# Taking the small extra matmuls out of attention and out of the output projection

## What is computed

```python
# attention, 16 heads of 64; n is normalised twice
xn = layernorm(layernorm(x)) * gamma
q, k, v = heads(xn @ Wq), heads(xn @ Wk), heads(xn @ Wv)
q, k = rotary(q) * 64 ** -0.5, rotary(k)
sim = q @ (k @ W_bilinear).T
x = x + merge(softmax(sim) @ v) @ Wo
# 8 experts, all computed for all tokens, two of them weighted in
xt = layernorm(x)
w, idx = top_k(xt @ Wg.T + bg, 2); w = softmax(w)
h = relu(xt @ W1[e].T + b1[e])
x = x + sum over e of comb[:, e] * (h @ W2[e].T + b2[e])
```

## Time and profile before

| what | value |
|---|---|
| median of 3 runs | 5789.53 us (5823.94, 5595.1, 5789.53) |
| profiled execution, its own time | 5596.39 us |
| its span on the slowest core | 5594.5 us (the eight cores: 5580.3 to 5594.5) |
| PE busy | 4492.4 us, 80% |
| ACT busy | 1806.0 us, 32% |
| DVE busy | 1051.8 us, 19% |
| mean granted TensorE clock | 0.707 of full |

### The profile page before, as it was taken

How to read it: one execution, slowest core, us unless ns; L and a number is a source line. 1 busy time by engine, 2 the same in 40 slices (tenths; PEclk the granted TensorE clock), 3 DMA queues, 4 the chain that set the end, 5 groups by cost and what they waited for, 6 DMA issues and landing times. The chain is left out here.

```text
span 5594.5 us, 49207 instructions; the slowest of 8 cores (5580.3 to 5594.5 us)
## 1 busy us (share of the span) xinstructions
PE 4492.4 (80%) x17554; PEld 1579.7 (28%) x17554; DVE 1051.8 (19%) x2222; ACT 1806.0 (32%) x2827; POOL 41.6 (1%) x66
## 2 busy tenths in 40 slices
PE   3445379999999543699999997529999999999999
PEld 1111112222222111122222222214444444444444
DVE  3343421000000334200000003440111111010101
ACT  1110135666656211266665662002121111212121
POOL 0000000000000000000000000000000000000000
PEclk8666655555555566655555555759999999999999
DMA  3223100000000232000000000600303203023031
GB/s 64 51 44 57 30 8 1 1 1 1 1 1 1 60 60 53 15 1 1 1 1 1 1 1 0 135 0 1 61 1 61 46 16 61 12 49 61 1 76 46
DMA packets 34702, 150.48 MB, mean 27 GB/s; under 512 B 2828, under 2 KB 2957, under 8 KB 32294
## 3 DMA queue, kind: packets, MB, share of 16 engines
q0 software_dynamic: 23952, 111.51, 11.6%
q1 hardware_dynamic: 10518, 35.83, 2.0%
HBM read 250.39 MB, written 8.39 MB: 46 GB/s over the span
## 5 line engine op out<-in xcount | busy, mean ns | idle before, releaser
L607 ACT ACTIVATE arena<-pb,arena 128x512 bf16<-128x512 f32 x2048 | 1287.4, 683 | 857.7 <-PE pb L596 857.7
L622 PE MATMUL pb<-arena 128*128 128x512 bf16 x2048 | 1246.1, 608 | 39.0 <-ACT arena L607 38.9
L970 PE MATMUL pb<-arena 128*128 128x512 bf16 x4096 | 894.0, 379 | 33.0 <-ACT arena L951 27.5
L944 PE MATMUL pb<-arena 128*128 128x512 bf16 x4096 | 891.2, 380 | 1.2 <-DMA arena<-w1t 1.1
L951 ACT ACTIVATE arena<-pb,arena 128x512 bf16<-128x512 f32 x512 | 351.8, 687 | 1446.9 <-PE pb L944 1446.9
L596 PE MATMUL pb<-arena 64*128 64x512 bf16 x2048 | 611.1, 605 | 0.0
L970 PEld LDWEIGHTS pb<-arena 128*128 128x128 bf16 x4096 | 396.4, 98 | 523.2 <-issue 54.2
L944 PEld LDWEIGHTS pb<-arena 128*128 128x128 bf16 x4096 | 400.4, 98 | 486.5 <-issue 5.7
L986 DVE SCALAR_TENSOR_TENSOR arena<-pb,arena 128x512 f32<-128x512 f32 x256 | 192.2, 751 | 1631.6 <-PE pb L970 1414.3
L626 PE MATMUL pb<-arena 1*1 1x64 bf16 x2048 | 424.0, 207 | 0.0
L640 DVE COPY arena<-pb 1x512 f32<-1x512 f32 x64 | 44.1, 689 | 1959.4 <-PE pb L622 1959.4
(11 more groups left out here) (136 smaller groups left out, 1522.5 us busy)
## 6 DMA issues: line engine op xcount, KB each, us to landing
arena<-wkv POOLq DMA_DIRECT2D x32, 1024.0 KB, 9.3
arena<-w1t POOLq DMA_DIRECT2D x8, 4096.0 KB, 27.2
arena<-w2t POOLq DMA_DIRECT2D x8, 4096.0 KB, 27.2
arena<-x_roll SPq DMA_DIRECT2D x48, 512.0 KB, 3.5
arena<-wq POOLq DMA_DIRECT2D x8, 1024.0 KB, 9.4
out<-arena SPq DMA_DIRECT2D x16, 512.0 KB, 2.6
arena<-wo POOLq DMA_DIRECT2D x1, 2048.0 KB, 20.4
arena<-costab SPq DMA_DIRECT2D x2, 512.0 KB, 5.2
```

The costliest lines, as they stand in the source:

```text
L607: l_exp = P.op("scalar", (lambda sb, pt, pr: lambda e: e.activation(out=pt, in_=pb[sb][:, :], func=AF.Exp, bias=s_bias[:, biascol + pr: bi ...
L622: e.matmul(pb[ob][0:128, :], a_v[:, js * VTW + h * (DH + 1): js * VTW + h * (DH + 1) + 128], pt, start=(js == 0), stop=(js == 15)),
L944: e.matmul(pb[b][:, :], f_w1[:, d * HID + hf * 128: d * HID + (hf + 1) * 128], f_ln2T[:, d * OWN + tc * 512: d * OWN + (tc + 1) * 512], st ...
L970: last = e.matmul(pb[b][:, :], f_hT[:, hf * 512 + m4 * 128: hf * 512 + (m4 + 1) * 128], f_w2[:, hf * D + oh * 512: hf * D + (oh + 1) * 512 ...
```

## The change

The small matmul behind each value matmul goes (two in each round, 2048 in all), and the one behind each group of the output projection (32 in all). The value matmul and the last matmul of a group still carry the signals. `warm_burst` stays. Nothing else differs; below L626 the changed file's lines have other numbers (L788 becomes L786).

```diff
-                            l_av = P.op("tensor", (lambda ob, h, pt, js: lambda e: (
+                            l_av = P.op("tensor", (lambda ob, h, pt, js: lambda e:
                                 e.matmul(pb[ob][0:128, :],
                                          a_v[:, js * VTW + h * (DH + 1):
                                              js * VTW + h * (DH + 1) + 128],
-                                         pt, start=(js == 0), stop=(js == 15)),
-                                e.matmul(pb[7][0:1, 0:64], c_ones128b[0:1, 0:1],
-                                         c_ones128b[0:1, 0:64], start=True,
-                                         stop=True))[0])(ob, h, pt, js),
+                                         pt, start=(js == 0), stop=(js == 15)))(
+                                             ob, h, pt, js),
...
-                lm = P.op("tensor", (lambda m, oh, b: lambda e: (
-                    [e.matmul(pb[b][:, :],
+                lm = P.op("tensor", (lambda m, oh, b: lambda e: [
+                    e.matmul(pb[b][:, :],
...
-                     for c in range(8)],
-                    e.matmul(pb[7][0:1, 0:64], c_ones128b[0:1, 0:1],
-                             c_ones128b[0:1, 0:64], start=True, stop=True))[0][-1])(m, oh, b),
+                    for c in range(8)][-1])(m, oh, b),
```

More of the change, by code:

```diff
@@ L786, in build_nc @@
                 b = (m * 2 + oh) % 4
-                lm = P.op("tensor", (lambda m, oh, b: lambda e: (
-                    [e.matmul(pb[b][:, :],
-                              a_aoT[:, c * OWN + m * 128: c * OWN + (m + 1) * 128],
-                              r_wo[:, c * D + oh * 512: c * D + (oh + 1) * 512],
-                              start=(c == 0), stop=(c == 7))
-                     for c in range(8)],
-                    e.matmul(pb[7][0:1, 0:64], c_ones128b[0:1, 0:1],
-                             c_ones128b[0:1, 0:64], start=True, stop=True))[0][-1])(m, oh, b),
+                lm = P.op("tensor", (lambda m, oh, b: lambda e: [
+                    e.matmul(pb[b][:, :],
+                             a_aoT[:, c * OWN + m * 128: c * OWN + (m + 1) * 128],
+                             r_wo[:, c * D + oh * 512: c * D + (oh + 1) * 512],
+                             start=(c == 0), stop=(c == 7))
+                    for c in range(8)][-1])(m, oh, b),
                     waits=[l_wo, bank_owner.get(b)], signal=L(tag))
```

## The result

| | before | after |
|---|---|---|
| median of 10 runs each | 5808.82 us (5595.07 to 5866.76) | 5045.56 us (4932.2 to 5356.96) |
| profiled execution | 5596.39 us | 4933.2 us |
| span of the slowest core | 5594.5 us | 4931.3 us |
| mean granted TensorE clock | 0.707 | 0.844 |

The account below looks back on a forecast made before the run. PE at half clock was taken to bound attention; 659 us from 64 blocks at 10.3 each and 8 us from the output projection, off 5596.4, gave 4930 us, range 4840 to 5300.

Parts of the forecast that it names:

- The bound: Attention: waits for PE at half clock, granted 0.50, with PE busy 94% and 33.39 us a block.
- The round at the low clock: Attention, one key tile: 1.90 us becomes 0.54 + 0.43 + 0.54 = 1.51 us, 0.39 less.
- bare-load rival: Attention at the low clock: weight loads stay bare, 0.28 us less a round, 287 + 8 gained, 5301 us; chance 0.06.
- The clock: Attention: denser full-height work raises the clock to 1.00 in most of each block; 4930 us, chance 0.62.
- rival of the low clock: Attention's clock stays low: gain 403 + 8 = 411 us, time 5185 us; chance 0.26.
- The round at full clock: Attention at 1.00: PE needs 0.89 us a round, so ACT's two exponentials bound it at 1.154 us.
- The loss at the change of blocks: Between attention blocks: 3.7 us at full clock, plus 0.9 us for a low-clock stretch, making 23.1 us a block.
- The low stretch: Attention, after most changes of blocks: 4 us of rounds at the low clock, costing 0.9 us a block.
- some 3 us: PE pauses this long at each change of blocks, so the clock will fall at most of these pauses.
- Output projection: Groups of eight L788 go from 1.95 to 1.70 us; 32 x 0.25 = 8 us gained, full clock kept.
- the rival on the slower side: Denser attention makes the experts' clock fall; at 0.75 they lose 606 us, time 5907 us; chance 0.03.

Follow-up runs that it names:

- run with small matmuls of full height: Kernel before, with the small matmul behind each value matmul given weights of 128 rows and 128 columns instead of one-row, one-column form; 4956.7 us.
- the two runs that kept one small matmul: Changed kernel with one small matmul a round put back: between the two value matmuls, 5261.2 us; between the second and the next scores, 4979 us by cores 0 to 3.
- projection's part alone: Kernel before, with only the 32 small matmuls L793 of the output projection taken out; 5591.2 us.
- run with 7 and 4 fillers: Changed kernel plus 7 full-height matmuls behind each block's last value matmul and 4 ahead of its first; 4858.9 us.
- run with the second small matmul kept: Changed kernel with the small matmul between the second value matmul and the next scores put back; 4979 us by cores 0 to 3.
- the full-height burst: Kernel before, with non-zero data in pass 0's one-row burst and 24 matmuls of 128 rows and 128 columns as pass 1's burst; 5581.6 us.

## Why the prediction was right, by its own steps

**The bound.** PE at a granted clock of 0.50 set attention's pace. With PE's work per round cut and its clock raised, the block fell from 33.37 to 23.17 us, and ACT took over in the rounds at full clock.

**The round at the low clock.** 1.51 us, forecast 1.51. Its parts are, by the median of the starts in the changed kernel's trace, 0.54 from the scores to L622, 0.40 to the second L622 and 0.56 to the scores, forecast 0.54, 0.43 and 0.54. The second L622's load is hidden: 0.40 us is no more than the 0.427 at which L449 follow each other at a granted clock of 0.50 (kernel before, 262.9 to 265.6 us). The bare-load rival is out. Equal shapes behave so in the run with small matmuls of full height too, where L622 takes 0.40 us to the matmul behind it. No run tells how the loads are hidden.

**The clock.** This was a judgement with a chance of 0.62, and it held; it falls at the changes of blocks as forecast, at 30 of 31. That one-row work does nothing for the clock, and that it is the form of the small matmuls and not their number that counts, is shown by two runs: full-height small matmuls leave the clock at 0.87, as without any, and a one-row burst leaves it at 0.50 with zeros as data and with others. That they act by the gaps they put between full-height work fits the two runs that kept one small matmul: with 1.65 us a round the clock mostly comes back, with 1.76 us only in part. It is not shown apart from the place of the small matmul. Of the full gain of 663 us, what the instructions cost at the low clock was forecast as 411 us (rival of the low clock). No run held the denser round at the low clock, so the split is by forecast alone; the low rounds measured at 1.51 us support it.

**The round at full clock.** 1.16 us, forecast 1.154. The spacings of 0.427 and 0.213 us for 512 columns were reckoned from GHz, while the traces give the clock as a share of full: they show 0.427 us at 0.50 (the L449 above) and 0.216 at 1.00 (L788, projection's part alone).

**The loss at the change of blocks.** Two terms were off, in opposite directions. The change itself is 3.2 us, forecast 3.7. Most of the difference is one reading: the 2.46 us from the end of L622 to the next scores came from rows at the low clock, and the eight transposes L647 in it are faster at the full one. Before, and in the run with 7 and 4 fillers, where they are L649:

```profile
809.23 0.98 PE L647 MATMUL pb<-arena 1*128 1x1 f32 x8 [1.41 <-DVE arena L641]
...
863.45 0.62 PE L649 MATMUL pb<-arena 1*128 1x1 f32 x8
...
864.01 0.61 PE L597 MATMUL pb<-arena 64*128 64x512 bf16 x4
```

From the transposes to the scores is 810.14 - 809.23 = 0.91 us before and 864.01 - 863.45 = 0.56 us at full clock, 0.35 us less. The low stretch costs 23.17 - 21.79 = 1.4 us a block, forecast 0.9: I took 4 us of rounds at the low clock, and 0.27 of a block is 6.3 us. About 0.2 us of the 1.4 lies in the change itself, where a low clock slows the transposes and the scores (4.19 us on average from the last exponential to the next block's first, 3.96 with the fillers); the rest lies in the rounds. PE's pause of "some 3 us" is two in the trace after, 1.61 us ahead of L645 and 0.61 us ahead of the first L622. Together 4.6 and 4.6. Here the forecast of 4930 had luck, about 0.5 us x 64 = 32 us in each direction.

**Output projection.** 6.0 to 6.5 us, forecast 8. The full clock was taken for all of it, and its first group or two run at the low one.

**The experts' clock.** They ran at 1.00 and 1818.7 us, so the rival on the slower side did not come true in the execution compared, nor in the run with 7 and 4 fillers, where attention has 1.00 throughout and the experts have it too. But a level between 0.50 and 1.00 exists: on core 6 of the run with the second small matmul kept, a stretch of the experts (PE alone) has 0.81, while cores 0 to 3 have 1.00 there.

```profile
3600.00:4000.00 400.00, 391.77 (x1471) 0.81 0.21 42
```

So the two levels of the earlier trace rows are not all that the experts can meet. No run here shows what brings the third, and attention's own clock on that core is 0.86, as on core 0.

## What to carry to other kernels

Fillers of the shape of the work beside them, 7 and 4 of 128 rows and 128 columns at a change of blocks, brought the share of full clock from 0.73 to 1.00. The one-row, one-column ones left it at 0.50, bared a weight load on each side (0.54 us ahead of one and 0.14 behind it, against 0.40 and 0.07 for the full-height form), and with two of them in each round the clock did not come back: together 663 us of 5596. Read starts, not durations, for what a small matmul costs (0.14 us to the next start here, at a mean duration of 0.21), and read the granted clock by stretch before and behind every pause: where it fell at one here, full-height work inside the pause was worth more than its time (4932 to 4859 us).

## What the runs showed of the hardware that I had not expected

The full clock, once there, lasted through over 20 us of work that raised it in no block: the first block of pass 1 behind the full-height burst, small matmuls included, kept 1.00, and the same block pattern stayed at 0.50 for the 1031 us after. And the turn between the two is not a step: at 1.76 us a round the same program on the eight cores took from 5199 to 5259 us, with mean clocks from 0.766 to 0.783.
